# States of a state-space scan written over their injections in SBUF, and twelve more rounds of injections made beside attention

## The reference

```python
dt = softplus(...)                      # [rows, 256]
A = -exp(Alog)                          # [256, 16]
def step(h, ins):
    dt_t, u_t, B_t, C_t = ins
    h = exp(dt_t[..., None] * A) * h + (dt_t * u_t)[..., None] * B_t[:, None, :]
    y_t = einsum('bdn,bn->bd', h, C_t)
    return (h, y_t)
y = (scan(step) + u * D) * silu(z)
out = y @ Wout.T
```

## Time and profile before

| what | us |
|---|---|
| median of 3 runs | 1311.38 |
| lowest and highest run | 1309.56, 1317.42 |
| the profiled execution | 1315.2 |
| its span, first to last instruction | 1313.5 |

### The profile page before, as it was taken

How to read it: one execution, slowest core, us unless ns; L and a number is a source line. 1 busy time by engine, 2 the same in 40 slices (tenths; PEclk the granted TensorE clock), 3 DMA queues, 4 the chain that set the end, 5 groups by cost and what they waited for, 6 DMA issues and landing times. The chain is left out here.

```text
span 1313.5 us, 18381 instructions
## 1 busy us (share of the span) xinstructions
PE 1038.3 (79%) x6017; PEld 340.7 (26%) x6017; DVE 1175.2 (89%) x1728; ACT 892.6 (68%) x1352; POOL 547.2 (42%) x395
## 2 busy tenths in 40 slices
PE   2789996888888888888888888884755977978764
PEld 1443331111111111111111111131411334544311
DVE  7892657999999999999999999838999999999997
ACT  6354558777777777777778887876645667677642
POOL 5030112502332023300000302326779999999896
PEclk9989996999999999999999999995656797787756
DMA  3034332314404464220000010016659676775452
GB/s 102 0 120 160 140 128 84 121 49 114 113 15 127 141 156 134 62 81 29 17 17 21 13 34 18 1 58 154 161 145 246 140 201 165 176 166 146 117 162 62
DMA packets 92386, 134.50 MB, mean 102 GB/s; under 512 B 15060, under 2 KB 45579, under 8 KB 92291
## 3 DMA queue, kind: packets, MB, share of 16 engines
q1 hardware_dynamic: 91266, 131.23, 36.2%
q0 software_dynamic: 1024, 2.10, 0.6%
HBM read 92.75 MB, written 40.24 MB: 101 GB/s over the span
## 5 line engine op out<-in xcount | busy, mean ns | idle before, releaser
L923 DVE TENSOR_REDUCE at_mpart<-psum 128x1 f32<-128x512 f32 x1024 | 637.9, 684 | 44.3 <-PE psum L1104 41.1
L895 ACT ACTIVATE at_probs<-psum 128x1024 f32<-128x1024 f32 x512 | 495.6, 1022 | 142.2 <-PE psum L1134 141.4
L1104 PE MATMUL psum<-at_ks,at_qs 56*128 56x512 bf16 x1024 | 203.0, 393 | 100.1 <-DVE at_mpart L923 99.3
L1147 PE MATMUL psum<-at_probs,at_vg 128*32 128x512 f32 x2048 | 274.8, 609 | 0.7 <-ACT at_probs L895 0.6
L1537 POOL TENSOR_TENSOR t_inject<-shared 128x1024 f32<-128x1024 f32 x92 | 215.5, 2353 | 29.4 <-POOLq L60 19.3
L742 POOL CAST at_m<-at_mneg 128x16 bf16<-128x16 f32 x16 | 4.0, 250 | 483.0 <-DVE at_mneg L928 476.0
L1609 ACT ACTIVATE psum<-shared,aneg 128x512 f32<-128x512 f32 x240 | 164.0, 690 | 51.9 <-DVE t_hc L1738 41.1
L1134 PE MATMUL psum<-at_qs,at_ks 59*128 59x512 bf16 x1024 | 157.4, 380 | 7.4 <-ACT at_probs L895 6.2
L1104 PEld LDWEIGHTS psum<-at_ks,at_qs 56*128 56x128 bf16 x1024 | 49.4, 93 | 424.2 <-DVE at_mpart L923 409.5
L1944 PE MATMUL psum<-t_hc,stack 128*32 128x512 f32 x480 | 94.0, 867 | 74.8 <-POOL t_hc L1522 48.5
L1522 POOL TENSOR_TENSOR t_hc<-t_hp,shared 128x512 f32<-128x512 f32 x100 | 125.9, 1269 | 33.8 <-DVE t_hp L1812 32.6
(11 more groups left out here) (262 smaller groups left out, 1150.1 us busy)
## 6 DMA issues: line engine op xcount, KB each, us to landing
shared<-mp_dt_d SPq DMA_DIRECT2D x64, 256.0 KB, 5.8
mp_ahead_d<-shared SPq DMA_DIRECT2D x7, 2048.0 KB, 7.9
t_ahead<-mp_ahead_d SPq DMA_DIRECT2D x28, 512.0 KB, 4.0
t_w<-in_w SPq DMA_DIRECT2D x46, 256.0 KB
shared<-mp_bc_d SPq DMA_DIRECT2D x152, 64.0 KB, 3.0
shared<-mp_dtu_d SPq DMA_DIRECT2D x36, 256.0 KB, 9.2
shared<-mp_dtu_d SPq DMA_DIRECT2D x56, 128.0 KB, 4.4
mp_u_d<-shared SPq DMA_DIRECT2D x8, 512.0 KB, 4.1
```

Of the source, the lines that this page charges most:

```text
L895: act.activation(probs[:, u_ % 2, p, :], s_pair[p], ACT.Exp, scale=float(HD) ** -0.5).then_inc(probs_ready, 1)
L923: dve.reduce_max(mpart[:, s % 2, 2 * jp + b, i, kc:kc + 1], ring[x % 3], AX.X).then_inc(ring_free, 1)
L1104: pe.matmul(ring[z_ % 3], qs[half(b, DQ), buf, of_pair(jp, c * CH + i * P, P)], ks[half(b, DQ), buf, of_pair(jp, kc * CH, CH)], start=True ...
L1147: mm = pe.matmul(o_bank[VW * j:VW * (j + 1), :], vg[:, g % 2, kt, j, :], probs[:, u_ % 2, j // 2, CH * (j % 2):CH * (j % 2 + 1)], start=(k ...
```

## The change

It does three things.

1. A scan writes its states over its own injections, in `inject` or `ahead` (both SBUF), for every tile: `states(k)`. The ring `hp` goes, and `inject` grows from 4 to 8 tiles (`NI`). VectorE's product with C now reads these states and `cs`, both in SBUF. Decays in PSUM are only read.
2. `AHEAD` becomes a list of groups: the seven blocks with all their rounds, and three pairs of blocks (6 and 7, 8 and 9, 10 and 11) with their rounds `q` 1 and 3. These are 12 more rounds (25, 27, ... 47) whose tiles 2 and 3 are made beside attention and loaded.
3. The weighings are dealt out anew: GpSimd takes tiles 0 and 1 first, and weighs two together where both are its own.

The waits change with it: ScalarE waits for the scan alone before it writes new decays; GpSimd waits until the old states in a slot of `inject` have been weighed and kept (`states_read`); SyncE does so before it loads into a slot of `ahead`.

```diff
-AHEAD = 1, 2, 3, 4, 13, 14, 15
+AHEAD = [((i,), range(NQ)) for i in (1, 2, 3, 4, 13, 14, 15)] + [((2 * n, 2 * n + 1), (1, 3)) for n in (3, 4, 5)]
+AHEAD_AT = {(i, q): (g, m * len(qs) + x) for g, (blocks, qs) in enumerate(AHEAD)
+            for m, i in enumerate(blocks) for x, q in enumerate(qs)}
...
-            return k // PB in AHEAD and k % NJ >= 2
+            return (k // PB, k // NJ % NQ) in AHEAD_AT and k % NJ >= 2
...
             if SCATTER <= r < SCATTER + MOVE or GATHER <= r < GATHER + MOVE:
-                return r // NQ in AHEAD and (j == 0 or j == 3 and r % 2 == 1)
-            if r // NQ in AHEAD:
-                return j in (0, 3) or j == 2 and (r < SCATTER or r % 2 == 1)
-            return j == 0 or j == 3 and r % 3 == 1
+                return is_ahead(NJ * r + 2) and (j == 0 or j == 1 and r % 2 == 1)
+            if is_ahead(NJ * r + 2):
+                return j < 2 or j == 2 and (r < SCATTER or r % 2 == 1)
+            return j == 0 or j == 1 and r % 3 == 1 and not is_ahead(NJ * r + 6)
...
+        def states(k, n=1):
+
+            if is_ahead(k):
+                x, j = ahead_rounds.index(k // NJ), k % NJ - 2
+                return ahead[:, x % NA, j:j + n, :]
+            x = by_inject[k] % NI
+            return inject[:, x:x + n, :]
...
                 if x >= NA:
-                    sp.wait_ge(scanned, NJ * (ahead_rounds[x - NA] + 1) - K0)
+                    done = ahead_rounds[x - NA] + 1
+                    sp.wait_ge(pool_weighed, by_pool[done])
+                    sp.wait_ge(dve_weighed, by_dve[done])
+                    sp.wait_ge(kept, keeps[NJ * done])
...
-                pool.tensor_tensor(hc[:, r % 2, j, :], hp[:, by_pool[k] % NHP, :], cs[:, (NQ * (i // NB) + q) % NBC, :],
-                                   ALU.mult).then_inc(pool_weighed, 1)
+                pool.tensor_tensor(hc[:, r % 2, j:j + n, :], states(k0, n),
+                                   cs[:, (NQ * (i // NB) + q) % NBC, :].unsqueeze(1).to_broadcast([P, n, CH]), ALU.mult)\
+                    .then_inc(pool_weighed, 1)
...
                     if x >= NI:
-                        pool.wait_ge(scanned, injected_tiles[x - NI + 1] + 1 - K0)
+                        states_read(injected_tiles[x - NI])
...
                 if k >= K0 + ND:
-                    if on_pool(k - ND):
-                        act.wait_ge(scanned, k - ND + 1 - K0)
-                    else:
-                        act.wait_ge(dve_weighed, part_of[k - ND])
-                    if keeps[k - ND + 1]:
-                        act.wait_ge(kept, keeps[k - ND + 1])
+                    act.wait_ge(scanned, k - ND + 1 - K0)
...
-                dve.tensor_tensor(hc[:, r % 2, j:j + n, :], decays[:, j:j + n, :],
+                dve.tensor_tensor(hc[:, r % 2, j:j + n, :], states(k0, n),
                                   cs[:, m % NBC, :].unsqueeze(1).to_broadcast([P, n, CH]), ALU.mult).then_inc(dve_weighed, 1)
...
-                dve.tensor_tensor_scan(h, decay[k % ND], added,
+                h = states(k)[:, 0, :]
+                dve.tensor_tensor_scan(h, decay[k % ND], h,
                                        last[:, k % PC:k % PC + 1] if n % NCH else 0.0, ALU.mult, ALU.add).then_inc(scanned, 1)
```

More of the change, by code:

```diff
@@ L701, in _ @@
                     first.load_steps(S, sp, s - 6, first_in[s - 4], 1)
[L702 removed]
+                if s == 12:
                     sp.wait_ge(a_st, 16 * len(AHEAD))
[L704 to L705 removed]
+                if 12 <= s < 15:
+                    for m in ((0, 1), (2, 3), (4,))[s - 12]:
+                        first.load_bc(S, sp, m, first_in[m + 6])
                 if s in (12, 13):
@@ L748, in split_max, with products @@
                 pool.tensor_tensor(m3[:, :, 2, :], mrem[:, :, :], m3[:, :, 1, :], ALU.subtract).then_inc(m3_ready, 1)
[L750 to L756, removed]
+            def products(g):
+                pool.wait_ge(a_in, 16 * SP4 * sum(len(blocks) + len(qs) for blocks, qs in AHEAD[:g + 1]))
+                if g:
+                    pool.wait_ge(a_st, 16 * g)
+                blocks, qs = AHEAD[g]
+                for m in range(len(blocks)):
+                    for x in range(len(qs)):
+                        pool.tensor_tensor(first.products[:, m * len(qs) + x, :, :], first.some_dus[:, m, :, :],
+                                           first.some_bs[:, x, :].unsqueeze(1).to_broadcast([P, 2, CH]), ALU.mult).then_inc(a_made, 1)
             def early_inject(p):
@@ L1252, in on_pool, with groups @@
             if SCATTER <= r < SCATTER + MOVE or GATHER <= r < GATHER + MOVE:
-                return r // NQ in AHEAD and (j == 0 or j == 3 and r % 2 == 1)
-            if r // NQ in AHEAD:
-                return j in (0, 3) or j == 2 and (r < SCATTER or r % 2 == 1)
-            return j == 0 or j == 3 and r % 3 == 1
[L1258 to L1262, removed]
+                return is_ahead(NJ * r + 2) and (j == 0 or j == 1 and r % 2 == 1)
+            if is_ahead(NJ * r + 2):
+                return j < 2 or j == 2 and (r < SCATTER or r % 2 == 1)
+            return j == 0 or j == 1 and r % 3 == 1 and not is_ahead(NJ * r + 6)
+        def groups(r, pool):
+            mine = [on_pool(NJ * r + j) == pool for j in range(NJ)]
+            parts = []
+            for j in (0, 2):
+                parts += [(j, j + 1)] if mine[j] and mine[j + 1] else [(x, x) for x in (j, j + 1) if mine[x]]
+            return parts
         ahead_rounds = [r for r in range(R0, NR) if is_ahead(NJ * r + 2)]
@@ L1268, in tail_stage @@
         injected_tiles = [k for k in range(K0, NK) if not is_ahead(k)]
-        by_pool, keeps = [0], [0]
-        pool_tiles = [k for k in range(K0, NK) if on_pool(k)]
+        keeps = [0]
         for k in range(NK):
-            by_pool.append(by_pool[-1] + (k >= K0 and on_pool(k)))
             keeps.append(keeps[-1] + (k >= K0 and k // PC % NCH < NCH - 1))
-        by_dve, part_of, ends_at = [0], {}, {}
+        by_dve, by_pool, part_of, ends_at = [0], [0], {}, {}
         for r in range(NR):
[L1276 to L1281, removed]
+            for by, pool_ in ((by_dve, False), (by_pool, True)):
+                of_round = groups(r, pool_) if r >= R0 else []
+                for n, (j0, j1) in enumerate(of_round):
+                    ends_at[NJ * r + j1, pool_] = NJ * r + j0
+                    for j in range(j0, j1 + 1):
+                        part_of[NJ * r + j] = by[-1] + n + 1
+                by.append(by[-1] + len(of_round))
         def chunk_at(r, shift):
@@ L1514, in weigh @@
             def weigh(k):
-                if k < K0 or not on_pool(k):
+                if (k, True) not in ends_at:
                     return
-                i, q, j = at(k)
-                r = k // NJ
+                k0 = ends_at[k, True]
+                i, q, j = at(k0)
+                r, n = k0 // NJ, k - k0 + 1
                 pool.wait_ge(scanned, k + 1 - K0)
@@ L1546, in _ @@
                         gather((k - GATHER * NJ) // 2)
-            for k in range(NK - NI + 1, NK):
+            for k in range(NK - LAG, NK):
                 weigh(k)
@@ L1614, in keep @@
                     return
[L1615 to L1621, removed]
+                act.wait_ge(scanned, k + 1 - K0)
+                act.activation(last[:, k % PC:k % PC + 1], states(k)[:, 0, CH - 1:CH], ACT.Copy).then_inc(kept, 1)
             def attended(c):
```

66 lines of the change are left out of this document (33 added, 33 removed).

## The result

The changed kernel takes 1382.01 us (median of 4 runs, 1381.58 to 1382.73) against 1311.71 us of the kernel before. The ratio is 1.0529, with a 95% interval of 1.0496 to 1.0563. It is 70 us slower. Slower was forecast, but 1343 us within 1302 to 1368: the loss is twice what I gave it, and outside the range.

A forecast was written before the change was run, and what follows sets the result against it. DVE and POOL together were taken to set the tail's pace; blocking +37 us less 5 for ACT gave +32, so 1315.2 + 32 = 1347 profiled, predicted median 1343 us, range 1302 to 1368.

The forecast's parts named there:

- The two in each other's way: Tail: DVE's two-SBUF products and POOL's instructions block each other, 0.95 us per meeting; +37 us after idle time and phases.
- the seven lines: Waits by stage of the tail: DVE's products times POOL's share times 0.95 us, from 3.3 to 30.8 us per stretch.
- turns without loss: Rounds 24-47: DVE and POOL alternate, +6 us, the lower end; as a rival for the whole kernel 1313 us, chance 0.16.
- Fewer injections: Rounds 24 to 47: twelve injections go; POOL has 10.1 us less work, DVE 9.2 us less, alone a gain of 9 us.
- Waits for ACT: Tail: ACT waits only for the scan before overwriting PSUM; of DVE's 15.8 us waiting for decays, 5 us come back.
- Loads: Twelve more loads of 512 KB for the tail, issued over a round ahead: 0, upper end 12 x 2 us.
- injections beside attention: Twelve products of 2357 ns and three stores moved into POOL's idle time beside attention: cost 0, 28 us if uncovered.
- the scan in place: Tail: DVE's scans writing to SBUF take as long as those in PSUM, 1274 against 1276 ns: 0.
- the product from SBUF by itself: Tail: DVE's product with two SBUF inputs, not held up, takes 1199 ns against 1205 from PSUM: 0.
- late loads: Rival: twelve tail rounds wait up to 2 us each for loads, 1367 us; chance 0.09 together with late sums.
- late sums: Rival: PE's sums come later and the gate waits, 15 gates x 1 us, 1358 us; chance 0.09 together with late loads.
- That the blocking costs little: Rival: POOL and DVE seldom meet or fall into step at once, so the gains stay, 1296 us; chance 0.09.

The follow-up runs named there:

- the first experiment: The changed kernel with VectorE's own tiles scanned over their decays in PSUM again and multiplied from there: 1318.26 us, 1.0031 of the kernel before.

## Why the prediction was right in kind and wrong in size

1. *The two in each other's way*: the mechanism was right. The trace of before showed it in three places, and it is what the changed kernel loses by: undone for DVE's products alone, 64 of 70 us go. The price of one meeting was right as well: a product that comes 0.12 us behind an injection takes 2.78 us, its 0.67 and 2.11, which is 2.35 less the 0.12 of its late start and the 0.12 of the earlier trace rows. On average a product took 0.93 us longer, inside the 0.5 to 1 us that I had named as the sign.
2. *The size of the waits* failed, in the stages with scatters and gathers above all. I set 65.2 us of waits (the sum of the seven lines before anything was taken off); the trace has 80.2. In rounds 12 to 19, 20 to 23 and 56 to 63 it was 15.2, 12.9 and 14.0 where I had 6.3, 6.0 and 7.1. There I had assumed, without a row for it, that an indirect DMA holds up no product. Three products that began beside one waited for the injection behind it as well, or for more (below); they alone lost 13.7 us. In rounds 24 to 47 the sum was 26.2 where I had 30.8, but that it came so near is luck: the 30.8 were for meetings at random, and the trace has one product in three at nearly the longest wait and the others at nearly none.
3. *What idle time and phases absorb* failed by as much. I took 19 us off: 10.4 for DVE's idle time, stage by stage, and 8.6 for phases that fit in rounds 24 to 47, where I chose the middle between turns without loss (+6) and the upper end (+21.6). The 5 us for ACT came on top, though those waits are part of the same idle time. So I had 15.4 us of idle time won back; it fell by 2.4 us in all, and in rounds 24 to 47 it rose by 6.1, because DVE then waited for late injections. That stretch grew by 24.3 us, beyond my upper end. The phases fitted for two products of three; the third came just behind the start of an injection, the worst moment, and again every second round. By the trace the sum is 80.2 us of waits, less 9.1 saved and 2.4 of idle time, 68.7 us, and the rounds grew by 67.3; I had 65.2, less 9.2, 19 and 5, 32 us.
4. *Fewer injections, a gain of 9 us*: wrong in size too. The work did shrink as reckoned (DVE 154.4 to 145.0), but the run with this part alone gained nothing, since it alternates POOL's load; with the products dealt to the even rounds the stretch gained 11.4 us. I had counted the engine's sum over 24 rounds, not in which round each instruction falls.
5. *Waits for ACT*, 5 us back: the size was right, they fell by 6.5 us (15.8 to 9.3). But the time was not gained, as waits for POOL's injections rose from 4.6 to 9.3 us:

```profile
DVE t_inject L1825 <- POOL t_inject L1568: 9.3, 7, 3.8
DVE t_inject L1825 <- ACT psum L1635: 5.3, 6, 1.2
DVE t_ahead L1825 <- ACT psum L1635: 4.0, 6, 1.5
```

6. *Loads, injections beside attention, the scan in place, the product from SBUF by itself*, all at 0: right. The product that meets nobody takes about 1193 ns for two tiles and 659 at the least for one, from PSUM 1205 and 666: 7 to 12 ns apart. The Trainium skill, VectorE: DVE Perf Modes, § The TRN2 errata, gives VectorE a fixed part of 58 cycles from SBUF and 120 from PSUM; the runs here do not show that difference for a product with two inputs.
7. The rivals: turns without loss did not occur. Neither did late loads (DVE waits for no landing) or late sums (DVE's gates wait for PE once, 2.1 us at the end, where it was 2.8 before). That the blocking costs little is refuted by the first experiment.

## What to carry to other kernels

Before an operand is moved from PSUM to SBUF, look whether the VectorE instruction then has two SBUF inputs while GpSimd is busy; here 86 such instructions cost 64 us. Where two engines shut each other out, do not take the wait from chance or let idle time absorb it: write out a period of both orders, price each product by where it meets the other engine, and look whether the other engine's results then come late. And in these runs work that was taken from an engine gained only where the rounds stayed even.

## What was not expected of the hardware

A waiting DVE instruction does not always get the next turn. The product at 1020.15 began while POOL's indirect DMA ran (1019.28 to 1020.29), and was passed by four POOL instructions, which all had their usual lengths; it ran only when POOL had nothing ready, at 1028.48, and took 9.42 us. First POOL, then DVE:

```profile
1019.28 1.01 POOL L1521 DMA_INDIRECT t_rows<-t_x,t_pos  x1 [0.15 <-issue]
1020.32 2.37 POOL L1568 TENSOR_TENSOR t_inject<-shared 128x1024 f32<-128x1024 f32 x1
1022.64 1.26 POOL L1543 TENSOR_TENSOR t_hc<-t_inject,shared 128x512 f32<-128x512 f32 x1
1023.86 4.62 POOL L1568 TENSOR_TENSOR t_inject<-shared 128x1024 f32<-128x1024 f32 x2
```

```profile
1020.15 9.42 DVE L1759 TENSOR_TENSOR t_hc<-t_ahead,shared 128x1024 f32<-128x1024 f32 x1
```

The run with the seven blocks alone shows the same instruction with 9.41 us, so it is no accident. I counted, over the changed kernel and the runs with seven blocks and with the later product, the products that began more than 0.14 us before the end of a POOL instruction with another right behind it. Behind an ordinary POOL instruction DVE had the next turn in 97 of 100 cases. Of ten such products beside an indirect DMA, seven were passed by the instruction behind it, and the other three were not held up at all. Why the seven lost stays open; the runs do not tell it. The other way round it is regular: in the run with the later product nine indirect DMAs began while a product had 0.92 or 0.93 us to go, and took 1.79 to 1.81 us, where 0.94 to 1.02 is usual. So the two do meet, which I had left out. The Trainium skill, SBUF — State Buffer, § Who interferes with whom, says that the engine that comes later is blocked for the whole instruction of the other: the 2.78 us product agrees, while the 9.42 us product was blocked for four more.
